# A full-array fp32 identity product before each maxima bank of an attention kernel on TensorE

## The reference

```python
Q, K, V = x @ Wq + bq, x @ Wk + bk, x @ Wv + bv      # 16 heads of 8 channels
attn = softmax(Q K^T / sqrt(8))                       # per sequence and head, 256 x 256
x = layernorm(x + (attn @ V) @ Wo + bo)
shared = (silu(x @ sw1) * (x @ sw3)) @ sw2            # hidden width 256
gates  = top-2 of sigmoid(x @ router_w.T) + router_bias, normalised
routed = sum over 8 experts of gate_e * (gelu(x @ ew1[e]) @ ew2[e])
out = layernorm(x + shared + routed)
```

## Time and profile before

| | us |
|---|---|
| median of 3 runs | 291.93 |
| lowest and highest of them | 290.07, 295.73 |
| the profiled execution | 290.25 |
| its span, first to last instruction | 288.5 |
| mean granted TensorE clock over the span | 0.81 of full |

### The profile page before, as it was taken

The page is one execution under the profiler, slowest core; times in us unless marked ns, Lnnn a source line. Parts: engine busy times, 40 slices in busy tenths (PEclk is TensorE's granted clock), DMA queues, the critical chain, the costliest instruction groups (busy, mean ns, idle before and its releaser), DMA issues.

```text
span 288.5 us, 4571 instructions
## 1 busy us (share of the span) xinstructions
PE 244.3 (85%) x1546; PEld 144.5 (50%) x1546; DVE 165.3 (57%) x372; ACT 142.7 (49%) x288; POOL 90.5 (31%) x180
## 2 busy tenths in 40 slices
PE   3799989168897978998889999998979999999980
PEld 2566544034464634555454554553756666566640
DVE  4665556248659657569668467022374655553853
ACT  2553459146677635557555447435458543434320
POOL 8309505140576214203313101404162534020201
PEclk9999999669799557569755556555799999999997
DMA  5302216722322440000294000272000016288111
GB/s 170 96 23 88 56 38 86 245 63 65 60 57 50 77 73 22 3 1 5 52 161 88 2 3 5 45 164 86 0 0 3 2 48 163 85 157 170 37 37 37
DMA packets 13687, 18.92 MB, mean 66 GB/s; under 512 B 1728, under 2 KB 6784, under 8 KB 13536
## 3 DMA queue, kind: packets, MB, share of 16 engines
q1 hardware_dynamic: 12560, 17.44, 27.3%
q10 hardware_dynamic: 720, 0.80, 0.8%
q0 software_dynamic: 384, 0.40, 0.4%
HBM read 11.74 MB, written 1.11 MB: 45 GB/s over the span
## 4 chain that ended last, share of the span: by engine, by line
PE 66%; SPq 10%; ACT 6%; DVE 5%; DMA 5%; issue 4%; POOL 1%; POOLq 0%; ACTq 0%; DVEq 0%
PE pv_bank L785 13%; PE ring L757 11%; PE max_bank L924 10%; SPq L295 7%; SPq L344 4%; ACT probs_mem L506 3%; PE max_bank L766 3%; PE misc_bank L832 3%; PE ring L730 2%; PE misc_bank L845 2%; PE ring L732 2%; PE ring L731 2%; DMA qstack<-top_rows 2%; PE max_bank L730 2%; PE max_bank L731 2%
## 5 line engine op out<-in xcount | busy, mean ns | idle before, releaser
L617 DVE TENSOR_REDUCE top<-max_bank 128x2 f32<-128x512 f32 x128 | 82.3, 683 | 37.4 <-PE max_bank L766 37.0
L506 ACT ACTIVATE probs_mem<-ring 128x512 f32<-128x512 f32 x128 | 72.2, 601 | 50.4 <-PE ring L757 48.7
L757 PE MATMUL ring<-qstack,kstack 26*128 26x256 f32 x256 | 56.4, 422 | 20.3 <-ACT probs_mem L506 11.9
L757 PEld LDWEIGHTS ring<-qstack,kstack 26*128 26x128 f32 x256 | 36.4, 253 | 42.3 <-ACT probs_mem L506 20.5
L766 PE MATMUL max_bank<-kstack,qstack 24*128 24x256 f32 x256 | 53.2, 421 | 3.5 <-DMA qstack<-gates_mem 1.8
L785 PE MATMUL pv_bank<-probs_mem,v 128*18 128x256 f32 x512 | 50.2, 529 | 0.5 <-ACT probs_mem L506 0.5
L766 PEld LDWEIGHTS max_bank<-kstack,qstack 24*128 24x128 f32 x256 | 34.3, 253 | 9.6 <-issue 3.4
L702 DVE TENSOR_TENSOR probs_mem<-probs_mem,gates_mem 128x512 f32<-128x512 f32 x32 | 22.5, 705 | 21.8 <-ACT probs_mem L578 18.8
L924 PE MATMUL max_bank<-probs_mem,wf 128*128 128x512 f32 x64 | 32.3, 591 | 0.0
L785 PEld LDWEIGHTS pv_bank<-probs_mem,v 128*18 128x18 f32 x512 | 14.4, 118 | 18.3 <-issue 12.6
L578 ACT ACTIVATE probs_mem<-ring 128x512 f32<-128x512 f32 x21 | 12.5, 596 | 19.9 <-PE ring L732 18.4
(11 more groups left out here) (132 smaller groups left out, 388.9 us busy)
## 6 DMA issues: line engine op xcount, KB each, us to landing
gates_mem<-gate_scratch SPq DMA_DIRECT2D x4, 2048.0 KB, 15.0
kstack<-gates_mem SPq DMA_DIRECT2D x36, 64.0 KB
qstack<-gates_mem SPq DMA_DIRECT2D x36, 64.0 KB
wf<-w_ffn_dram SPq DMA_DIRECT2D x1, 1408.0 KB, 8.3
qstack<-top_rows SPq DMA_DIRECT2D x64, 4.0 KB
out_dram<-xs SPq DMA_DIRECT2D x4, 256.0 KB, 2.7
xs<-x_dram SPq DMA_DIRECT2D x3, 256.0 KB, 7.4
probs_mem<-w_first_dram ACTq DMA_DIRECT2D x1, 384.0 KB, 6.0
```

What stands on the lines that cost most here:

```text
L506: nc.scalar.activation(probs[:, tick % 2, c, :], ring[k % NRING][:, :], ACT.Exp, scale=SCALE).then_inc(probs_made, 1)
L617: dve.tensor_reduce(top[:, n % 2, (c + 2) % HPS, i % 2, :], max_bank[m % NMAX][:, :].rearrange("p (h k) -> p h k", h=2), AX.X, ALU.max).th ...
L757: ins = mm(ring[(4 * i + c) % NRING][:, kt * S:(kt + 1) * S], kstack[r, t, b * S + kt * P:b * S + (kt + 1) * P], qstack[r, t, b * S:(b + 1 ...
```

## The change

One line at the end of `wait_for_maxima`: for every step and every `c`, after the waits of the maxima bank and before its first product, an fp32 product of the identity with itself over all 128 rows and 128 columns into the first 128 columns of that maxima bank. The bank's first product, `maxima(i, c, 0)`, has `start=True` and writes over it. The line runs 128 times, 4 for each of 32 steps, and nothing reads what it writes.

```diff
                 if n >= NMAX:
                     pe.wait_ge(max_taken, n - NMAX + 1)
+
+                mm(max_bank[n % NMAX][:, 0:P], ident[:, :], ident[:, :], start=True, stop=True)
```

## The result

| | before | changed |
|---|---|---|
| median, us | 292.13 (4 runs) | 376.43 (4 runs) |
| lowest and highest, us | 290.07, 295.73 | 370.41, 393.40 |
| profiled execution, us | 290.25 | 370.41 |
| its span, us | 288.5 | 368.7 |

The forecast of "slower" holds, 376 us lies in the range of 340 to 465, and the point of 415 us is 39 us too high.

A forecast was written before the change was run, and what follows sets the result against it. TensorE's own sequence was taken to bound the kernel, with VectorE setting the pace at the full clock. 290.25 profiled + 113 in steps 0 to 27 + 14 ahead = 417, given as 415 us median; range 340 to 465.

The forecast's parts named there:

- The mechanism: Attention steps: each identity product pays its own slot and splits the row-group block, adding 5.3 us low, 3.1 us full per step.
- change of kind: TensorE switching between full-array and row-group products, claimed to drain the array: 0.13 us low, about 0.1 us full.
- The entry of a half tick: Lone first score product plus the switch to the identity product: 0.50 us low, 0.31 us full.
- VectorE's share: Sign to look for: VectorE's busy share falling to near 40% in the attention.
- The slack: TensorE's idle time per step, all swallowed by the additions: 0.44 us at 1.2 GHz (low), 0.7 us at 2.4 GHz (full).
- The projections: Two later units within steps 0 to 27, some 6 us low or 3.5 us full each: + 10 us.
- The mix of levels: Steps 0 to 27: two thirds of the time at the 0.50 clock, against 59% before.
- rival (a): Clock held at the full level nearly throughout by frequent full-array work, step costs unchanged: 340 us, chance 0.17.
- Ahead of the attention: Ticks -4 to -1: 16 added products at the low level, + 17 us, 3 hidden in load waits: + 14.
- (c): Change of kind not paid: identity's weight load is pulled ahead and row groups still overlap; 310 us, chance 0.05.
- (d): Identity products fill TensorE's idle time, keeping the clock up, with no change of kind paid: 280 us, faster, chance 0.03.
- Theory L: From the follow-up experiments: how much of the time TensorE streams decides the clock level, which decides the time.

## Why the prediction was right, and where it was off

**The mechanism held.** Inserted products change the kind of work twice and cut the block, at 1.44 us low and 0.84 us full from one to the next: measured 1.44 and 0.85. The two kernels that remove the change of kind (301.8 us) or gather it at the half tick's edge (283.1 us) lose 11 us and nothing. How large the loss gets is decided by the level as well: with the same distance of 0.85 us from one to the next, the kernel with the product ahead of the scores takes 303.3 us. The rule that a change of tiling mode drains TensorE, which the prediction cited from the Trainium skill (TensorEngine Tiling (Array Packing), Key Properties), agrees with these rows: from the last row-group start to the next identity product it is 0.34 us at the low level (196.06 - 195.72) and 0.21 at the full one (152.87 - 152.66). The entry of a half tick, 0.31 and 0.50, measured 0.30 and 0.51. VectorE's share fell to 45%, "near 40%". The rest of the kernel is unchanged, 88.0 us against 87.9.

**The slack was sized too small.** "0.44 per step low, 0.7 full" took the time in which the engine is not busy. A busy TensorE includes the modelled ends of its matmuls, which the front part of this document warns of, so the true slack was larger. One full step of the kernel before shows it, from the `times_v` at 129.15 us to the next:

```profile
131.14 0.28 PE L757 MATMUL ring<-qstack,kstack 26*128 26x256 f32 x1
...
132.09 0.38 PE L757 MATMUL ring<-qstack,kstack 26*128 26x256 f32 x1 [0.68 <-ACT probs_mem L506]
...
132.86 0.38 PE L757 MATMUL ring<-qstack,kstack 26*128 26x256 f32 x1 [0.26 <-ACT probs_mem L506]
...
133.30 1.06 PE L785 MATMUL pv_bank<-probs_mem,v 128*18 128x256 f32 x16
```

The profile counts 0.94 us idle (0.68 + 0.26). But from 131.14, the last start of one half tick, the next half tick's block would need 0.21 + 0.43 us, and it is 2.16 us to the next `times_v` (133.30 - 131.14): 1.5 us of slack. A full step grew by 1.5 us (3.94 to 5.46) where 3.1 - 0.7 = 2.4 was forecast, and a low one by 4.4 (5.65 to 10.05) where 5.3 - 0.44 = 4.9 was. The prediction also names VectorE as what sets the pace at the full level; the waits that TensorE shows there are for ScalarE's exponentials (ACT, L506). Two of its sums are loose, and small beside this: 3.94 - 0.7 + 3.1 is 6.3 and not 6.4, and 417 us stands for 419 at the median, where 415 was said.

**The projections were counted on top.** "+ 10 us" for two later units. Steps 0 to 27 came to 224 us with them, against 254 forecast; 28 = T (0.64 / 10.05 + 0.36 / 5.46) with the measured steps and share gives 216 us, and leaves 8 for the projections and the waits for DMA, where the forecast had 13. The two terms, step lengths and this one, make up the 30 us. The rest of the distance between the 417 us of the sum and the 370 of the profiled execution stands ahead of the attention and in the last four steps, below.

**The mix of levels was right in number, without a reason that would carry.** Two thirds low was forecast, 64% measured. But the argument (the same share of streaming before and after, so the same returns) can't tell this order from the one with the product ahead of the scores, which spends a tenth of its time low. The forecast's value was lucky in that sense. The level also moves between executions of the changed kernel: its mean clock over the span was 0.777 in the shortest (370.41 us) and 0.703 in the longest (393.40 us). The profile's busy time gives no hint either: TensorE is busy for 222.71 of 224.00 us and yet 64% of the time at the low level.

The lower bound, 340 us for rival (a), all at the full level, was too high for the same reason as the steps: 28 steps of 5.46 us, with the 8 us above and the measured rest of the kernel (37.0, 19.7 and 88.0), make some 306 us. The kernel with the product ahead of the scores, at a mean clock of 0.95, took 303.3. Had the changed kernel kept the level as that one did, its time would have fallen out of the range. That the doubled kernel takes 344 us is no support for the 340: it has twice the inserted work, and its 28 steps take 196.40 us against (a)'s 189.

**Ahead of the attention**, 14 us were forecast and 3.2 measured. The change of kind is there (timeline, low level: identity product, block of maxima, identity product):

```profile
11.68 0.79 PE L754 MATMUL max_bank<-ident 128*128 128x128 f32 x2 [1.07 <-DVE kstack L634]
12.40 0.79 PE L768 MATMUL max_bank<-kstack,qstack 24*128 24x256 f32 x2
13.12 0.80 PE L754 MATMUL max_bank<-ident 128*128 128x128 f32 x2
...
23.83 0.49 PE L754 MATMUL max_bank<-ident 128*128 128x128 f32 x2
24.25 0.50 PE L768 MATMUL max_bank<-kstack,qstack 24*128 24x256 f32 x2
...
34.85 1.16 PE L840 MATMUL misc_bank<-wa,xt 128*128 128x128 f32 x8
35.85 0.39 PE L754 MATMUL max_bank<-ident 128*128 128x128 f32 x2
```

1.44 us from 11.68 to 13.12 as forecast. But from 23.83 us on an identity product takes 0.42 us to the next kind in place of 0.72, and the eight instructions of L840 that take 2.01 us before take 1.00 us (35.85 - 34.85): this part came to the full level, which the forecast had at the low one throughout, and which the kernel before reaches at about 42 us. In the last four steps, forecast as unchanged, the clock is 0.71 where it was 0.50, and they give back 4.3 us.

**Rivals.** (c), the change of kind is not paid, is refuted by the timelines. (d), faster because the level is kept up, has a true half: the level can be kept up by such products, and the kernels that do it outside the block are faster than before, by 5%. Its condition, under 0.3 us for each product at the full level, is met there (two steady distances of 0.11 us) and not in the change's place.

## What to carry to other kernels

On TensorE, price an inserted product by the distances between starts around it, with the change of kind on both sides and the row-group block that it cuts, and not by its own streaming; put it where work of its kind already stands. Where TensorE runs at two levels, the level is part of the price: a filler in the right place can pay for itself, and removing or shrinking work in the wrong place need not gain anything. Take slack from the distances too, since busy time includes modelled ends.

## What the runs showed of the hardware

- Doubling an inserted full-array product made a kernel 32 us faster (376 to 344 us), since the mean clock in the attention rose from 0.68 to 0.94; with half of it (one instruction in place of two) nothing was gained (373 us) and the clock was at 0.61.
- The same number of full-array products, 0.85 us apart in both kernels, ran 64% of the time at the low level with a lone row-group product ahead of each pair, and 10% without.
- An added product on 24 rows, without a change of kind, went with a lower level (0.63 against 0.73, or 0.70 with the stretch up to 42 us read as low), where full-array products at the half tick's edge went with a higher one (0.88 to 0.90). Theory L forecast the doubled kernel and the small fillers well, but taken by itself it would expect the product on 24 rows to raise the level. That the rows in use matter would fit both, but no run varies them alone; what decides the level stays open.
- Fillers on the full array, put behind other full-array work, cost two distances of 0.11 us each in a full-level step where they stood ahead of a tick's second half, and nothing where they stood ahead of its first half, in which TensorE waits for the exponentials (4.35 us a step with three ahead of the second half, 3.90 with one or two ahead of the first and one ahead of the second, 3.68 with none).
